# Decay exponents of a Mamba-2 layer made on ScalarE from running sums, instead of on TensorE from split rows

## The chip, the cores and the metric

One Trainium2 chip, one of its cores. The metric is the device time of one execution in microseconds. PE is TensorE, DVE is VectorE, ACT is ScalarE, POOL is GpSimd, SP the engine that issues most transfers.

## What is computed

A Mamba-2 block (1024 tokens = 4 batches of 256, 512 features, 128 heads of 64, 8 groups with a state of 128) and after it a quantised feed-forward block. What matters here, cut from the reference:

```python
A_dt = (dt * A).reshape(b, nc, CHUNK, H).transpose(0, 3, 1, 2)
A_cum = jnp.cumsum(A_dt, axis=-1)
L = jnp.exp(_segsum(A_dt))
Y_diag = jnp.einsum('bzlhn,bzshn,bhzls,bzshp->bzlhp', Cc, Bc, L, xch)
decay_states = jnp.exp(A_cum[..., -1:] - A_cum)
states = jnp.einsum('bzlhn,bhzl,bzlhp->bzhpn', Bc, decay_states, xch)
...
Y_off = jnp.einsum('bzlhn,bzhpn,bhzl->bzlhp', Cc, prev, jnp.exp(A_cum))
Y = (Y_diag + Y_off).reshape(b, s, H, P) + hs * D[None, None, :, None]
```

For each head, batch and chunk of 128 tokens one needs the matrix exp(sum_l - sum_s) for l >= s (a chunk with itself, called own below) and for the second chunk the same against the first chunk's tokens (past). It is multiplied with C.B, which all 16 heads of a group share, to M, and y = M times x.dt.

## The kernel before

The channels go in 64 tiles of 128 (2 heads each), 8 tiles to a group. Each engine runs its own program of `step`s (one a tile) and, after the 8 tiles of a group, a `window` (the group's output projection and the next group's B and C); semaphores tie the engines. There is no planner: on each engine the order is that in which the code is written, so an instruction that waits holds all behind it on its engine. `over_tiles` writes the loops out; inside a group two tiles make one loop body.

In the step of a tile PE transposes hs (`turn`, 2 halves), projects the next tile's hs and gate in four units of 12 matmuls of 512 columns (`unit`: 0 and 1 are hs, 2 and 3 the gate, each a half of the tokens; numbers are held as two fp32r parts, so three matmuls make one), makes the exponents (`exponents`, six matmuls of 512 columns, on rows that hold the running sums as three bf16 parts), and makes y (`y_first`, `y_second`, 16 and 32 matmuls of 128 columns as the profile counts them). ACT makes the last tap of the convolution (`tap3`), the tanh of each silu (`hs_tanh`, `gate_tanh`), the exponentials (`decay`, `decays`: for a chunk's own matrix a Relu first, which bounds the exponent, then Exp) and the upper parts of weights (`upper_pair`: casts of w_raw, two a tile; `wo_hi`). DVE does the other three taps (`conv_rest`), the products of the silus (`hs_silu`, `gate_silu`), x.dt (`times_dt`), M (`weigh`, six of 512 columns) and hs.D + y. POOL makes the lower parts of weights, gated, its squares and their sum.

The proj banks tie them: unit 2 of PE takes the bank of unit 0, and so waits until DVE has done `conv_rest(0)`; unit 0 of the next tile waits for `gate_silu(0)`. SP loads wo_raw when POOL has split the last one, then the rows, then the pair of w_raw.

Ahead of the first tile, dt is projected, turned, and put through softplus; PE sums dt.A (L808), ACT copies the sums and splits them with POOL into three bf16 parts (L592 to L612), SP stores these, and loads each tile's rows back.

## Time and profile before

| | |
|---|---|
| median of 3 runs | 1919.47 us (1918.16 to 1920.56) |
| profiled execution: its time, its span | 1918.38 us, 1916.6 us |
| PE busy | 1820.9 us, 95% |
| DVE busy | 1301.1 us, 68% |
| POOL busy | 1006.9 us, 53% |
| ACT busy | 918.7 us, 48% |
| granted TensorE clock, mean | 0.986 |

Busy time is what an engine's instructions take; the span runs from the first instruction to the last. Matmuls overlap in the pipeline, so PE's pace is read from their starts, not from their durations. The profile's page gives shares, its timeline the order in time, and its chain the work that ended last.

### The profile page before, as it was taken

Reading aid. Unit: us, or ns where it says so; the run is one execution under the profiler, and the core shown is the slowest. Engines: PE = TensorE matmul, PEld = TensorE weight load, DVE = VectorE, ACT = ScalarE, POOL = GpSimd, SP = SyncE. Lnnn points to the kernel's source line nnn. Section 1 sums busy time; section 2 is a strip of 40 time slices with the busy share of each in tenths; the row PEclk is TensorE's granted clock in tenths of the full one; section 3 lists DMA queues with packets and bytes.
Section 4 is the critical chain, followed back from the end, with each engine's and each line's share of the span. In section 5 each row is a group of like instructions: output and inputs, shape, how many; then the busy total and the mean of one; then the engine's idle time right before and its main releaser. Section 6 shows DMA issues by size and latency. Waiting matters only on the chain.

```text
span 1916.6 us, 37316 instructions
## 1 busy us (share of the span) xinstructions
PE 1820.9 (95%) x11192; PEld 1484.7 (77%) x11192; DVE 1301.1 (68%) x2149; ACT 918.7 (48%) x1660; POOL 1006.9 (53%) x802
## 2 busy tenths in 40 slices
PE   5799999999999999999999999999999977989898
PEld 4677787778777877787778777877887756878887
DVE  6588638863886388638863886388648857777776
ACT  3566536643664366436643664366436632212221
POOL 4266636663666366536653666366636665233220
PEclk9899999999999999999999999999999988999999
DMA  2211101110111011101110111011101110111101
GB/s 91 61 52 51 34 12 51 51 33 12 51 51 33 12 51 51 33 12 51 51 33 12 51 51 33 12 51 51 33 12 52 40 48 20 41 44 36 40 11 45
DMA packets 43639, 74.90 MB, mean 39 GB/s; under 512 B 10356, under 2 KB 11508, under 8 KB 43608
## 3 DMA queue, kind: packets, MB, share of 16 engines
q1 hardware_dynamic: 42600, 73.12, 12.1%
q10 hardware_dynamic: 1008, 1.38, 0.2%
...
q14 instruction: 14, 0.11, 0.0%
...
## 4 chain that ended last, share of the span: by engine, by line
PE 87%; DVE 8%; issue 2%; POOL 1%; ACT 1%; DVEq 0%; POOLq 0%; ACTq 0%
PE proj L743 15%; PE proj L745 15%; PE proj L744 15%; PE y L875 6%; PE y L929 6%; PE y L931 5%; PE y L930 5%; PE y L865 3%; PE trb L842 3%; PE diff L851 3%; DVE gated L1234 2%; PE misc L851 1%; PE y L743 1%; PE y L744 1%; PE y L745 1%
## 5 line engine op out<-in xcount | busy, mean ns | idle before, releaser
L743 PE MATMUL proj<-xhi,w_hi 128*128 128x512 f32 x1088 | 465.9, 428 | 5.6 <-DVE v L1057 5.6
L745 PE MATMUL proj<-xhi,w_lo 128*128 128x512 f32 x1088 | 425.9, 391 | 0.0
L744 PE MATMUL proj<-xlo,w_hi 128*128 128x512 f32 x1088 | 425.6, 391 | 0.0
L392 POOL TENSOR_TENSOR w_lo<-w_raw,w_hi 128x512 fp32r<-128x512 f32 x144 | 184.2, 1298 | 227.9 <-ACT w_hi L522 227.9
L1057 DVE SCALAR_TENSOR_TENSOR v<-proj,par_sb,v 128x510 f32<-128x510 f32 (+2 forms) x384 | 281.9, 741 | 15.0 <-ACT v L544 11.7
L448 POOL TENSOR_TENSOR g_lo<-gated,g_hi 128x512 fp32r<-128x512 f32 x128 | 164.8, 1290 | 190.4 <-ACT g_hi L675 189.8
L743 PEld LDWEIGHTS proj<-xhi,w_hi 128*128 128x128 f32 x1088 | 205.0, 188 | 75.2 <-issue 7.9
L745 PEld LDWEIGHTS proj<-xhi,w_lo 128*128 128x128 f32 x1088 | 204.8, 188 | 46.4
L744 PEld LDWEIGHTS proj<-xlo,w_hi 128*128 128x128 f32 x1088 | 205.4, 189 | 38.6
L1152 DVE TENSOR_TENSOR M<-diff,cb 128x512 f32<-128x512 f32 x256 | 170.1, 686 | 81.4 <-ACT diff L630 81.4
L929 PE MATMUL y<-wo_hi,g_hi 128*128 128x512 f32 x512 | 204.3, 399 | 5.5 <-POOL g_lo L448 5.1
L930 PE MATMUL y<-wo_lo,g_hi 128*128 128x512 f32 x512 | 201.2, 393 | 0.0
L931 PE MATMUL y<-wo_hi,g_lo 128*128 128x512 f32 x512 | 201.1, 393 | 0.0
L416 POOL TENSOR_TENSOR wo_lo<-wo_raw,wo_hi 128x512 f32 (+1 forms) x64 | 81.9, 1279 | 223.9 <-ACT wo_hi L658 223.9
L675 ACT CAST g_hi<-gated 128x512 fp32r<-128x512 f32 x128 | 78.6, 620 | 236.7 <-PE y L931 236.7
L544 ACT ACTIVATE v<-proj,par_sb 128x512 f32<-128x512 f32 x128 | 99.7, 779 | 188.6 <-PE proj L745 188.6
L626 ACT ACTIVATE diff<-diff 128x512 f32<-128x512 f32 x192 | 105.5, 579 | 136.9 <-PE diff L851 136.9
L1197 DVE SCALAR_TENSOR_TENSOR resid<-y,rg,resid 128x512 f32<-128x512 f32 x64 | 47.9, 749 | 170.5 <-PE y L931 169.0
L424 POOL TENSOR_TENSOR gated<-hs,gate 128x512 f32 (+1 forms) x128 | 162.7, 1292 | 0.4 <-DVE hs L1178 0.4
L438 POOL TENSOR_TENSOR sqacc<-sqacc,sq 128x512 f32<-128x512 f32 x128 | 162.6, 1291 | 0.0
L875 PEld LDWEIGHTS y<-M,xdt 128*64 128x64 f32 x2048 | 110.5, 137 | 25.5 <-issue 22.2
L875 PE MATMUL y<-M,xdt 128*64 128x128 f32 x2048 | 125.9, 276 | 2.8 <-DVE M L1152 2.8
...
## 6 DMA issues: line engine op xcount, KB each, us to landing
w_raw<-in_win SPq DMA_DIRECT2D x144, 256.0 KB, 2.7
wo_raw<-in_wout SPq DMA_DIRECT2D x64, 256.0 KB, 2.6
M<-in_w SPq DMA_DIRECT2D x14, 512.0 KB, 3.3
cb<-in_w SPq DMA_DIRECT2D x7, 512.0 KB, 3.3
...
out<-resid SPq DMA_DIRECT2D x8, 256.0 KB, 2.0
...
resid<-in_x SPq DMA_DIRECT2D x4, 256.0 KB, 4.6
```

Of the source, the lines that this page charges most:

```text
L392: e.tensor_tensor(w_lo[:, slot, i, :], w_raw[:, i, :], w_hi[:, slot, i, :].bitcast(F32), ALU.subtract).then_inc(split.sem, 1)
L424: e.tensor_tensor(gated[:, bass.ds(j, 1), h * HALF:(h + 1) * HALF], hs[:, par_:par_ + 1, h * HALF:(h + 1) * HALF], gate[:, par_:par_ + 1, ...
L448: e.tensor_tensor(g_lo[:, kk, :, :], gated[:, 4 * kk:4 * kk + 4, t * P:(t + 1) * P], g_hi[:, kk, :, :].bitcast(F32), ALU.subtract).then_in ...
L743: e.matmul(o, hi_l, hi_r, start=first, stop=False)
L744: e.matmul(o, hi_l, lo_r, start=False, stop=False)
L745: return e.matmul(o, lo_l, hi_r, start=False, stop=last)
L875: mm = e.matmul(ybank[b // 2][head * HD:(head + 1) * HD, (b % 2) * S + P:(b % 2 + 1) * S], xdt[:, 2 * b + part, head * HD:(head + 1) * HD] ...
L929: e.matmul(o, g_hi[:, kk, k, :], wo_hi[:, kt, :], start=first, stop=False)
L930: e.matmul(o, g_hi[:, kk, k, :], wo_lo[:, kt, :], start=False, stop=False)
L931: mm = e.matmul(o, g_lo[:, kk, k, :], wo_hi[:, kt, :], start=False, stop=last)
L1057: e.scalar_tensor_tensor(dst[:, :, d:S], src[:, :, 0:S - d], weights(K - 1 - d), dst[:, :, d:S], ALU.mult, ALU.add)\
L1152: e.tensor_tensor(M[:, SLOT[q], :], dbank[q % 3][:, :], cb[:, q // 2, :], ALU.mult)\
```

## The change

The running sums stay fp32 and go to HBM once; each tile gets two rows of them (one a head), each broadcast over 128 partitions by the transfer itself (`load_row`, 128 x 1024 fp32), and a block of 24 columns (`load_offset`) with each partition's own sum, for every block of 128 tokens. ACT forms the exponent as it reads the row: `decay_own` makes eight Relu of 128 columns with the offset as bias and one Exp over 1024 columns, `decay_past` four Exp of 128 columns with bias. PE's exponent matmuls go. DVE weighs an own matrix in one operation of 1024 columns. Head 0 of a tile is made and weighed a tile ahead (for a group's first tile, in the window before it), head 1 in the tile. y is one block after unit 1. The two own banks are now one tensor of 1024 columns. Ahead of the first tile B and C are projected before hs and gate, and the splitting of the sums is gone. POOL keeps one buffer of squares in place of two.

```diff
-        M = sb("M", [P, 4, HALF])
-        bc = M[:, :, :].rearrange("p (a u) f -> p a (u f)", a=2)
+        M = sb("M", [P, 6, HALF])
+        bc = M[:, 0:4, :].rearrange("p (a u) f -> p a (u f)", a=2)
+        M_own = [M[:, a:a + 2, :].rearrange("p a f -> p (a f)") for a in (0, 4)]
+        M_past = [M[:, 2, :], M[:, 3, :]]
...
+
+            def load_row(t, head):
+                sp.dma_start(row[:, head, :],
+                             sums[bass.ds(2 * t + head, 1), :].rearrange("a f -> (a f)").partition_broadcast(P))\
+                    .then_inc(s_row[head], 16)
+
+            def load_offset(t, par_):
+                sp.dma_start(offset[:, par_, :], offsets[:, bass.ds(t, 1), :].rearrange("p a k -> p (a k)"))\
+                    .then_inc(s_row[0], 16)
...
+            def step(g, j, par_, nxt, nxt2, ahead):
                 sp.wait_ge(wolo.sem, wolo.at(g, j, 0))
                 sp.dma_start(wo_raw[:, :], wout[TPG * g + j, :, :]).then_inc(woraw.sem, 16)
                 if nxt:
-                    sp.wait_ge(dready.sem, dready.at(g, j, 1))
-                    load_rows(TPG * g + j + 1, 1 - par_)
+                    sp.wait_ge(edone.sem, edone.at(g, j, 2))
+                    load_offset(TPG * g + j + 1, 1 - par_)
+                    load_row(TPG * g + j + 1, 0)
                 if nxt2:
                     load_pair(9 * g + j + 3, split.at(g, j, 0))
+                if nxt:
+                    sp.wait_ge(edone.sem, edone.at(g, j, 4))
+                    load_row(TPG * g + j + 1, 1)
 
...
+            def decay_own(g, j, par_, head):
+
+                act.wait_ge(s_row[head], (16 * TPG * (2 - head)) * g + (32 - 16 * head) * j + 16)
+                act.wait_ge(mdone.sem, mdone.at(g, j, 2 * head - 1))
+                for z in range(2):
+                    for b in range(B):
+                        block = 2 * b + z
+                        at = head * NB + block
+                        ins = e.activation(diff[z][:, b * P:(b + 1) * P], row[:, head, block * P:(block + 1) * P],
+                                           ACT.Relu, scale=-1.0, bias=offset[:, par_, at:at + 1])
+                ins.then_inc(dbound.sem, 1)
+                act.wait_ge(dbound.sem, dbound.at(g, j, head + 1))
+                e.activation(own[:, :], own[:, :], ACT.Exp, scale=-1.0).then_inc(edone.sem, 1)
+
+            def decay_past(g, j, par_, head):
+
+                act.wait_ge(mdone.sem, mdone.at(g, j, 2 * head))
+                for b in range(B):
+                    block = 2 * b + 1
+                    at = head * NB + 2 * B + b
+                    ins = e.activation(misc[:, b * P:(b + 1) * P], row[:, head, block * P:(block + 1) * P],
+                                       ACT.Exp, bias=offset[:, par_, at:at + 1])
+                ins.then_inc(edone.sem, 1)
+
+            act.wait_ge(s_off, 6)
+            act.wait_ge(cbd.sem, cbd.at(0, 0, 0))
+            decay_own(0, 0, 0, 0)
+            decay_past(0, 0, 0, 0)
+
+            def step(g, j, par_, nxt, nxt2, ahead):
+                decay_own(g, j, par_, 1)
+                decay_past(g, j, par_, 1)
                 w = tile_weights(TPG * g + j + 1)
                 if nxt:
                     tap3(0, w, ready.at(g, j, 1), silu.at(g, j, -1))
-                decay(2)
-                decay(3)
+                if nxt2:
+                    act.wait_ge(ready.sem, ready.at(g, j, 0))
+                    upper_pair(par_, 9 * g + j + 3)
                 if nxt:
                     tap3(1, w, ready.at(g, j, 2), silu.at(g, j, 0))
                     act.wait_ge(gdone.sem, gdone.at(g, j, 0))
                     hs_tanh(hs[:, 1 - par_, :], 0, taken.at(g, j, 1))
-                if nxt2:
-                    act.wait_ge(ready.sem, ready.at(g, j, 0))
-                    upper_pair(par_, 9 * g + j + 3)
-                decays(4)
+                if ahead:
+                    decay_own(g, j + 1, 1 - par_, 0)
                 if nxt:
                     hs_tanh(hs[:, 1 - par_, :], 1, taken.at(g, j, 2))
+                if ahead:
+                    decay_past(g, j + 1, 1 - par_, 0)
+                if nxt:
                     gate_tanh(gate[:, 1 - par_, :], 0, ready.at(g, j, 3))
                 act.wait_ge(woraw.sem, woraw.at(g, j, 16))
                 act.wait_ge(gused.sem, gused.at(g, 0, 0))
                 e.activation(wo_raw[:, :], wo_raw[:, :], ACT.Copy,
                              scale=par_sb[:, bass.ds(TPG * g + j, 1), K + 2:K + 3].rearrange("p a b -> p (a b)"))\
                     .then_inc(woscaled.sem, 1)
-                if nxt:
-                    gate_tanh(gate[:, 1 - par_, :], 1, ready.at(g, j, 4))
                 act.wait_ge(woscaled.sem, woscaled.at(g, j, 1))
                 e.copy(wo_hi[:, bass.ds(j, 1), :].rearrange("p a f -> p (a f)"), wo_raw[:, :])\
                     .then_inc(wohi.sem, 1)
+                if nxt:
+                    gate_tanh(gate[:, 1 - par_, :], 1, ready.at(g, j, 4))
                 if not nxt:
 
                     for h in range(2):
                         act.wait_ge(gdone.sem, gdone.at(g, j, h + 1))
-                        act.wait_ge(sacc.sem, sacc.at(g, j, h - 1))
-                        e.activation(sq[:, h:h + 1, :], gated[:, bass.ds(j, 1), h * HALF:(h + 1) * HALF],
-                                     ACT.Square).then_inc(sqs.sem, 1)
+                        act.wait_ge(sacc.sem, sacc.at(g, j, h))
+                        e.activation(sq[:, :], gated[:, bass.ds(j, 1), h * HALF:(h + 1) * HALF]
+                                     .rearrange("p a f -> p (a f)"), ACT.Square).then_inc(sqs.sem, 1)
 
             def window(g, nxt):
...
@@ -683,6 +679,10 @@
                     bc_tile(g + 1, 1, ready.window(g, 0), taken.window(g, 0), silu.window(g, 0))
                 for i in range(2, 16):
                     g_upper(i)
+                    if i == 12 and nxt:
+                        act.wait_ge(cbd.sem, cbd.at(g + 1, 0, 0))
+                        decay_own(g + 1, 0, 0, 0)
+                        decay_past(g + 1, 0, 0, 0)
                     if i == 7 and nxt:
...
 
             def first_unit(n):
 
+
                 pair, piece, h = n // 4, (n // 2) % 2, n % 2
 
-                free = (None, None, 1, 2, None, None, 3, 4)[n]
-                project(pair, piece, h, 2 * pair + piece + 1, free, bc_banks[0][piece] if pair else proj)
...
+                def y():
+                    pe.wait_ge(mdone.sem, mdone.at(g, j, 4))
                     pe.wait_ge(xdts.sem, xdts.at(g, j, 2))
                     pe.wait_ge(ysum.sem, ysum.at(g, j, 0))
                     pe.wait_ge(oadded.sem, oadded.at(g, 0, 0))
                     for b in range(B):
-                        for head in range(2):
-                            mm = e.matmul(ybank[b // 2][head * HD:(head + 1) * HD, (b % 2) * S:(b % 2) * S + P],
-                                          xdt[:, 2 * b, head * HD:(head + 1) * HD],
-                                          M[:, SLOT[head], b * P:(b + 1) * P], start=True, stop=True)
-                    mm.then_inc(yready.sem, 1)
-
...
+
+                        for z, part in ((0, 0), (1, 0), (1, 1)):
                             for head in range(2):
+                                weights = M_past[head][:, cols] if z > part else \
+                                    M_own[head][:, after_own if z else cols]
                                 mm = e.matmul(
-                                    ybank[b // 2][head * HD:(head + 1) * HD, (b % 2) * S + P:(b % 2 + 1) * S],
-                                    xdt[:, 2 * b + part, head * HD:(head + 1) * HD],
-                                    M[:, SLOT[2 + 2 * part + head], b * P:(b + 1) * P],
-                                    start=(part == 0), stop=(part == 1))
+                                    ybank[b // 2][head * HD:(head + 1) * HD,
+                                                  (b % 2) * S + z * P:(b % 2) * S + (z + 1) * P],
+                                    xdt[:, 2 * b + part, head * HD:(head + 1) * HD], weights,
+                                    start=(part == 0), stop=(part == z))
                         if b % 2:
                             mm.then_inc(yready.sem, 1)
 
                 turn(0)
-
-                pe.wait_ge(s_rowq[par_], (TPG * 32) * g + 32 * j + (64 - 32 * par_))
-                pe.wait_ge(cbd.sem, cbd.at(g, 0, 0))
-                exponents(0)
-                exponents(1)
                 if nxt:
                     unit(0)
                 turn(1)
-                exponents(2)
-                exponents(3)
                 if nxt:
                     unit(1)
-                y_first()
-                exponents(4)
-                exponents(5)
+                y()
                 if nxt:
                     unit(2)
                     unit(3)
-                y_second()
 
             def window(g, nxt):
...
+            def weigh_own(g, j, head):
+                dve.wait_ge(edone.sem, edone.at(g, j, 2 * head + 1))
+                if head == 0:
+                    dve.wait_ge(cbd.sem, cbd.at(g, 0, 0))
+                    dve.wait_ge(yready.sem, yready.at(g, j, 0))
+                e.tensor_tensor(M_own[head], own[:, :], cb[:, 0:2, :].rearrange("p a f -> p (a f)"), ALU.mult)\
+                    .then_inc(mdone.sem, 1)
+
+            def weigh_past(g, j, head):
+                dve.wait_ge(edone.sem, edone.at(g, j, 2 * head + 2))
+                e.tensor_tensor(M_past[head], misc[:, :], cb[:, 2, :], ALU.mult).then_inc(mdone.sem, 1)
+
+            weigh_own(0, 0, 0)
+            weigh_past(0, 0, 0)
+            gate_silu(gate[:, 0, :], 0, 7)
+            gate_silu(gate[:, 0, :], 1, 8)
+
+            def step(g, j, par_, nxt, nxt2, ahead):
                 t = TPG * g + j
                 y = hs[:, par_, :]
 
@@ -1143,40 +1150,30 @@
                     scale = dt[:, 4 * h:4 * h + 4, bass.ds(2 * t, 2)].unsqueeze(3).broadcast_to([P, 4, 2, HD])
                     e.tensor_tensor(dst, src, scale, ALU.mult).then_inc(xdts.sem, 1)
 
...
                 times_dt(0)
-                weigh(0)
-                weigh(1)
+                weigh_own(g, j, 1)
                 times_dt(1)
-                if nxt:
-                    conv_rest(0, w, tap.at(g, j, 1), convs.at(g, j, 0),
-                              (lambda: weigh(2), lambda: weigh(3)))
+                weigh_past(g, j, 1)
+                if nxt:
+                    conv_rest(0, w, tap.at(g, j, 1), convs.at(g, j, 0))
                     conv_rest(1, w, tap.at(g, j, 2), convs.at(g, j, 2),
                               (lambda: hs_silu(hs[:, 1 - par_, :], 0, tanh.at(g, j, 1)),))
-                else:
-                    weigh(2)
-                    weigh(3)
-                weigh(4)
-                weigh(5)
+                if ahead:
+                    weigh_own(g, j + 1, 0)
                 if nxt:
                     hs_silu(hs[:, 1 - par_, :], 1, tanh.at(g, j, 2))
                     gate_silu(gate[:, 1 - par_, :], 0, tanh.at(g, j, 3))
+                if ahead:
+                    weigh_past(g, j + 1, 0)
+                skip = tile_weights(t)
+                for h in range(2):
+
+                    dve.wait_ge(yready.sem, yready.at(g, j, h + 1))
+                    e.scalar_tensor_tensor(halves(y, h), halves(y, h), skip(K + 1), ybank[h][:, :],
+                                           ALU.mult, ALU.add).then_inc(ysum.sem, 1)
+                if nxt:
                     gate_silu(gate[:, 1 - par_, :], 1, tanh.at(g, j, 4))
-                own = tile_weights(t)
-                for h in range(2):
-
-                    dve.wait_ge(yready.sem, yready.at(g, j, h + 2))
-                    e.scalar_tensor_tensor(halves(y, h), halves(y, h), own(K + 1), ybank[h][:, :],
-                                           ALU.mult, ALU.add).then_inc(ysum.sem, 1)
 
             def window(g, nxt):
                 if nxt:
@@ -1198,6 +1195,9 @@
                                            ALU.mult, ALU.add).then_inc(oadded.sem, 1)
                     if t == 3 and nxt:
                         cbs_kept(cbr.window(g, 1))
+                    if t == 6 and nxt:
+                        weigh_own(g + 1, 0, 0)
+                        weigh_past(g + 1, 0, 0)
                     if not nxt:
                         dve.wait_ge(oadded.sem, oadded.window(g, t + 1))
                         moments(t)
```

ACT's program, in the middle of a step (hs is the tile's silu input, v the convolution, diff and misc the exponents' banks). Before, it reads:

```order
L555 ACTIVATE hs<-v 128x512
L644 REGISTER_ALU
L521 ISA
L522 CAST w_hi<-w_raw 128x512 x2
L625 REGISTER_ALU
L626 ACTIVATE diff<-diff 128x512
L625 REGISTER_ALU
L626 ACTIVATE misc<-misc 128x512
L629 REGISTER_ALU
L630 ACTIVATE diff<-diff 128x512
L629 REGISTER_ALU
L630 ACTIVATE misc<-misc 128x512
```

and in the changed kernel, from the same hs tanh (L535 here), where own and misc are the exponents' banks and row and offset their sources:

```order
L535 ACTIVATE hs<-v 128x512
L598 ISA
L599 ISA
L604 ACTIVATE own<-row,offset 128x128 x8
L607 ISA
L608 ACTIVATE own<-own 128x1024
L535 ACTIVATE hs<-v 128x512
L612 REGISTER_ALU
L616 ACTIVATE misc<-row,offset 128x128 x4
L538 REGISTER_ALU
L539 ACTIVATE gate<-proj 128x512
```

The casts of w_raw have moved from behind the first hs tanh to a place ahead of the second tap; behind that tanh now stand the nine activations of the next tile's head 0, with its past block behind the second hs tanh.

DVE's program from the start of a step: M products, x.dt and the first conv steps. Before:

```order
L1152 TENSOR_TENSOR M<-diff,cb 128x512
L1138 REGISTER_ALU
L1144 ISA
L1144 TENSOR_TENSOR xdt<-trb,dt 128x512
L1052 ISA
L1057 ISA
L1057 SCALAR_TENSOR_TENSOR v<-proj,par_sb,v 128x2x255
L1147 REGISTER_ALU
L1152 TENSOR_TENSOR M<-misc,cb 128x512
L1056 ISA
L1057 ISA
L1057 SCALAR_TENSOR_TENSOR v<-proj,par_sb,v 128x2x254
```

and in the changed kernel:

```order
L1151 TENSOR_TENSOR xdt<-trb,dt 128x512
L1124 ISA
L1128 TENSOR_TENSOR M<-own,cb 128x1024
L1145 REGISTER_ALU
L1151 ISA
L1151 TENSOR_TENSOR xdt<-trb,dt 128x512
L1132 REGISTER_ALU
L1133 TENSOR_TENSOR M<-misc,cb 128x512
L1036 ISA
L1041 ISA
L1041 SCALAR_TENSOR_TENSOR v<-proj,par_sb,v 128x2x255
```

Before, M products stand between the conv steps of half 0; now both of head 1 (1024 and 512 columns) stand ahead of the first of them, with `times_dt(1)` between.

SP's transfers of a step. Before:

```order
L305 ISA
L306 ISA
L306 DMA wo_raw<-in_wout 128x512
L308 ISA
L281 ISA
L281 DMA row_r<-rows_r 3x2048
L283 ISA
L283 DMA row_l<-rows_l 4x768
L283 ISA
L283 DMA row_l<-rows_l 4x768
L283 ISA
L283 DMA row_l<-rows_l 4x768
```

and in the changed kernel:

```order
L286 ISA
L286 DMA offset<-offsets 128x24
L281 ISA
L281 DMA row<-sums 128x1024
L273 ISA
L274 ISA
L274 DMA w_raw<-in_win 128x512
L273 REGISTER_ALU
L274 ISA
L274 DMA w_raw<-in_win 128x512
L309 REGISTER_ALU
L281 ISA
L281 DMA row<-sums 128x1024
```

Four small loads have given way to the offset block and a row ahead of the w_raw pair, and a second row behind it.

## Rows read from the trace of the kernel before

**Rows 1.** The page's first part: busy us, share of the span, instructions.
```profile
PE 1820.9 (95%) x11192; PEld 1484.7 (77%) x11192; DVE 1301.1 (68%) x2149; ACT 918.7 (48%) x1660; POOL 1006.9 (53%) x802
```

**Rows 2.** PE's timeline in one tile: start us, us, engine, line, operation, count.
```profile
912.56 0.66 PE L842 MATMUL trb<-ident,hs 128*128 128x128 f32 x4
...
920.98 0.39 PE L851 MATMUL diff<-row_r,row_l 128*128 128x512 bf16 x1
...
921.65 0.40 PE L744 MATMUL proj<-xlo,w_hi 128*128 128x512 f32 x1
```

**Rows 3.** The chain that ended last: start us, us, what; the y matmuls of two tiles.
```profile
97.45 1.90 PE y L875 x32
...
195.63 1.90 PE y L875 x32
```

**Rows 4.** ACT's timeline in the tile that PE begins at 912.56.
```profile
916.97 0.78 ACT L544 ACTIVATE v<-proj,par_sb 128x512 f32<-128x512 f32 x1 [1.45 <-PE proj L745]
917.65 0.59 ACT L620 ACTIVATE misc<-misc 128x512 f32<-128x512 f32 x1
...
921.80 1.13 ACT L522 CAST w_hi<-w_raw 128x512 fp32r<-128x512 f32 x2
...
924.30 0.56 ACT L630 ACTIVATE misc<-misc 128x512 f32<-128x512 f32 x1
924.78 0.63 ACT L555 ACTIVATE hs<-v 128x512 f32<-128x512 f32 x1
925.30 0.60 ACT L559 ACTIVATE gate<-proj 128x512 f32<-128x512 f32 x1
925.78 0.73 ACT L652 ACTIVATE wo_raw<-wo_raw,par_sb 128x512 f32<-128x512 f32 x1
```

**Rows 5.** ACT's timeline ahead of the first tile: 128 and 1024 columns.
```profile
25.73 0.31 ACT L532 ACTIVATE sq<-sq 128x128 f32<-128x128 f32 x1
...
34.87 1.06 ACT L567 ACTIVATE gated<-gated 128x1024 f32<-128x1024 f32 x1
35.83 0.76 ACT L544 ACTIVATE v<-proj,par_sb 128x512 f32<-128x512 f32 x1
```

**Rows 6.** DVE's timeline: three conv steps in a row, and two M products.
```profile
39.21 2.31 DVE L1057 SCALAR_TENSOR_TENSOR v<-proj,par_sb,v 128x510 f32<-128x510 f32 x3
...
924.50 0.69 DVE L1152 TENSOR_TENSOR M<-diff,cb 128x512 f32<-128x512 f32 x1 [0.44 <-ACT diff L630]
925.11 0.68 DVE L1152 TENSOR_TENSOR M<-misc,cb 128x512 f32<-128x512 f32 x1
```

**Rows 7.** Timelines of ACT, POOL, DVE and PE late in one window.
```profile
1030.13 0.62 ACT L675 CAST g_hi<-gated 128x512 fp32r<-128x512 f32 x1 [2.10 <-PE y L931]
1032.85 0.62 ACT L675 CAST g_hi<-gated 128x512 fp32r<-128x512 f32 x1 [2.10 <-PE y L931]
...
1030.83 1.28 POOL L448 TENSOR_TENSOR g_lo<-gated,g_hi 128x512 fp32r<-128x512 f32 x1 [1.44 <-ACT g_hi L675]
...
1032.94 0.75 DVE L1197 SCALAR_TENSOR_TENSOR resid<-y,rg,resid 128x512 f32<-128x512 f32 x1 [4.69 <-PE y L931]
...
1038.10 0.60 PE L842 MATMUL trb<-ident,hs 128*128 128x128 f32 x4
```

**Rows 8.** PE's timeline ahead of the first tile and in it.
```profile
75.98 0.77 PE L824 MATMUL diff<-M 128*128 128x128 f32 x2 [11.14 <-DVE M L1071]
...
80.95 0.60 PE L842 MATMUL trb<-ident,hs 128*128 128x128 f32 x4
83.24 0.60 PE L851 MATMUL diff<-row_r,row_l 128*128 128x512 bf16 x2 [1.68 <-DVE cb L1127]
```

**Rows 9.** SP's timeline in the tile of 912.56; transfers: KB, median us to landing.
```profile
916.24 0.98 SPq L275 DMA_DIRECT2D w_raw<-in_win  x2
...
w_raw<-in_win SPq DMA_DIRECT2D x144, 256.0 KB, 2.7
...
M<-in_w SPq DMA_DIRECT2D x14, 512.0 KB, 3.3
```

298 lines of the change are left out of this document (121 added, 177 removed).

## Prediction

> **What bounds the kernel now.** First the page's busy shares [rows 1]: TensorE (PE) is busy 95% of the span, VectorE (DVE) 68%, ScalarE (ACT) 48%, so a first look says that only PE's own work counts. Then PE's timeline in one tile [rows 2]: its pieces follow each other without a gap. From the first exponent matmul at 920.98 to the second matmul of the next projection at 921.65 are 0.67 us for two exponents and one 512-column projection matmul; twelve of those take 2.72 in the stretch of [rows 7], 0.23 each, so two exponents cost 0.44. Then the chain that ended last [rows 3]: six tiles between 97.45 and 195.63 give **16.36 us a tile**. ACT and DVE have slack inside it: but the question for this change is how much, since it puts work on ACT.
>
> **What it takes from PE.** Six exponent matmuls a tile, 3 x 0.44 = 1.32 us, and one of the two seams around the y matmuls, about 0.1. The 24 y matmuls stay. PE alone would need 16.36 - 1.42 = 14.95 us a tile.
>
> **What it puts on ACT.** Gone are ten 512-column activations. They come at 0.48 to 0.52 us from start to start (924.30, 924.78, 925.30 in [rows 4]), 4.95 us in all. New are 24 activations of 128 columns with a bias from SBUF (16 Relu, 8 Exp) and two Exp of 1024.
>
> The slot s of a small one is the number on which everything hangs, and before has none like it. From rows: a Tanh from SBUF has a slot of 0.52 (924.78 to 925.30), and 1024 columns have 0.96 (34.87 to 35.83, [rows 5]), so 384 columns fewer are 0.33 less: 0.19. An operand pointer costs extra: the Identity with scale and bias from SBUF has 0.68 (916.97 to 917.65), 0.20 over the plain 0.48 from PSUM, so 0.10 each. s = 0.19 + 0.10 = **0.29**. Lower bound: the plain fixed part may be that of the Exps on PSUM (0.48 less 0.43 for the columns, 0.05), then s = 0.11 + 0.05 + 0.10 = 0.26, and 0.25 with a cheaper pointer. Upper bound: the one 128-column activation of before lasts 0.31 us [rows 5]; with the pointer and no overlap 0.41, with 0.09 of overlap 0.32. I take 0.29, since both of its parts come from back-to-back rows.
>
> The Trainium skill (ScalarE: Activation LUTs, What ACT_TABLE_LOAD costs) gives 280 ns + 0.833 ns a column with a pointer bias, and about 93 ns of overlap back to back; that is an estimate of 0.294 us for this instruction, by which the sum below would be some 4 us longer. The rows of before have no such instruction to confirm it.
>
> ACT's content is then: the rest of a tile (two taps 0.68, two hs tanh 0.52, two casts of w, two gate tanh 0.48, the wo scaling 0.76 and cast 0.52) 5.6, plus 24 x 0.29 = 7.0, plus 2 x 0.92 (an Exp of 0.48 with 0.43 more columns), plus 0.12 twice, where Exp waits for the last Relu of its own and the overlap is lost: **14.7 us**. That alone nearly fills 14.95, and ACT also waits.
>
> **The ring.** One path now goes round once a tile, by the order in which the code stands. Head 1: Relus 2.32 + 0.12; Exp 0.99 and 0.10 to reach DVE; weigh_own of 1024 columns 1.14 (a 512-column one has 0.61, 924.50 to 925.11; at most twice that, 1.22, and 0.07 or so of it is fixed, [rows 6]); times_dt 0.60; weigh_past 0.60; then the three conv steps of half 0, which nothing interleaves any more, 2.31 [rows 6] and 0.10 back to ACT; hs tanh 0.52; head 0 of the next tile: Relus 2.32 + 0.12, Exp 0.92; hs tanh 0.52; four past Exps 1.16; gate tanh 0.48; wo scaling 0.76, wo cast 0.52; gate tanh 0.50; the loop's branch and registers 0.10; and head 1 of the next tile. Sum **16.20 us**, = 10.40 + 20 s. PE is not on it: its units 2 and 3 wait for the conv results, its y for weigh_past. So the steady tile goes from 16.36, bound by PE, to 16.20, bound by ACT and DVE in turn. What covered ACT's work before was PE's length; it is used up.
>
> Not every tile pays the ring. In a window ACT and DVE are idle much of the time; head 0 of the coming tile is made there, and head 1 can start when DVE has weighed it: the output addition at 1032.94 [rows 7] + 0.75 + 1.14 = 1034.9, 3.2 us ahead of the tile's start at 1038.10. The first tile of a group therefore goes at PE's 14.95, the second at about 15.35 (the lead is used up in it: its tap waits for PE's unit 0), six at 16.20. A group: 127.5 against 8 x 16.36 = 130.9, **-3.4 x 8 = -27 us**.
>
> **The window.** ACT casts one g_hi per 2.72 us (1030.13 to 1032.85), POOL's half ends at 1030.83 + 1.28 = 1032.11, and PE wants it at 1032.85 - 0.1: 0.6 of slack [rows 7]. Between the 13th and the 14th cast now stand head 0's activations, 12 x 0.29 + 0.12 + 0.92 = 4.5. The 14th comes at 0.53 + 4.5 = 5.0 instead of 2.72, PE stands 1.7 to 1.8: **+12.5 us** in seven windows.
>
> **Ahead of the first tile.** B and C are now projected first, the exact three-part split (three rounds of casts, negations and POOL subtractions) and its twelve stores are gone. Before, PE waits 11.14 us for B and C and begins C.B at 75.98; the tile's first projection starts after 83.24, at 83.5 [rows 8]. After, DVE's queue sets it. From 39.21 [rows 6]: two half convs 4.44, two steps of the dt chain at 1.25 (1024 columns and the wait for each other) 2.5, two silus 1.3, the clip 0.7 and the product with A 1.25, which gives 49.4; C's convs 4.44 and silus 1.3, 55.1; a wait of 0.4 for v; hs convs 4.44, 60.0. C.B at its old length (80.95 - 75.98), 65.2; three copies and lags 67.2; ACT's head 0 3.5 and lag, 70.8; weigh_own 1.14, weigh_past 0.6, gate silu 0.6: 73.2. That is the unit's start, **-10.3 us**. POOL's memsets of the rows fall away ahead of the first norm too, which may give 1 or 2 us more; they are not in the sum. The row and offset transfers (issued near 58 to 64) are hidden by the C.B part; without that cover they would cost 3 to 5 us once.
>
> **DMA.** Each tile now loads two rows over 128 partitions, 512 KB each, and a small offset block, in place of four small loads. SP's order matters: wo_raw, offset, row of head 0, then the pair of w_raw, which before was issued at 916.24, 3.7 us into its tile, and landed 2.7 later [rows 9]. ACT's casts of it stood 9.2 us into the tile (921.80) and are moved ahead of the second tap. Now wo_raw is issued when POOL has split the previous tile's wo, whose cast ends about 1.2 us into the tile: + 1.3 + 0.4 = 2.9; w_raw at 4.9 and 5.4; behind 512 KB (3.3 to land against 2.7 for 256 KB, [rows 9], so 0.6 for each further 256 KB) it lands at 8.0 and 8.6. The casts then end near 9.1 and the tap near 9.8, where hs tanh would start by the ring at 9.8. So it is hidden, with nothing to spare: I cost it at 0. The second row (issued 6.3, needed at the tile's end) has about 7 us. POOL keeps its work and its slack.
>
> The last stage is unchanged. Sum: -27 + 12.5 - 10.3 = -25, from the profiled execution's own 1918.4 (span 1916.6, median of the runs 1919.5, 1.1 above it): **1893 us**.
>
> **The rivals.**
> *PE stays the bound* (s at 0.23 or less, or shorter waits than I sum). For: PE's rows without gaps, and s is derived, not seen. Against: all rows on pointers and on SBUF sources. 64 x -1.42 = -91, windows +6, ahead -10: 1823. Chance 0.12; the ground between it and the forecast (s near 0.25, tile 15.4: -0.8 x 48, with the second tiles and windows -45) gives 1848, 0.18.
> *w_raw comes late, slower than before.* The casts stand ahead of the second tap in ACT's queue; if the second piece lands x later than 8.7 us into the tile, tap, hs tanh and everything behind them shift by x, and all but the first tiles pay, 56 x. At x = 0.5 the gain is gone; at x = 1, 1893 + 56 = 1949. For: 1.3 MB in a burst on one queue, a row read 128 times from the same 4 KB. Against: the landing times of before, at low DMA load [rows 9]. Chance 0.10.
> *The small activations are slower than 0.31* (no full overlap when each reads a pointer): s = 0.32 gives a tile of 16.8, +0.6 x 48 + 2: 1924; s = 0.41, 2010. Chance 0.10.
> *No net change*, ring and windows eating the gain ahead of the first tile: 1916 to 1923, 0.06, at s = 0.31 to 0.32.
>
> **How the numbers follow.** The forecast with its own spread (s 0.27 to 0.305, 0.1 of lags in the ring, 1870 to 1910) has 0.44. Each 0.01 us of s moves the time by 10 us, each 0.1 us of wait in the ring by 5. The range leaves out the PE-bound end and the far slow end: 1843 to 1928. 0.2% (3.8 us) is what a measurement of this kernel tells from no change. Faster: 0.12 + 0.18 + 0.44 + a share of the slower cases that end below = 0.78; same 0.06; slower 0.16.
>
> **What would show it.** ACT busy over 80%, with 128-column activations at 0.36 to 0.39 us each and 0.29 from start to start; PE under 93%, waiting once a tile for DVE (y for M, or a transpose for xdt) by 1.2 us in all, in tiles 3 to 8 of a group and not in the first; a stand of 1.8 us before the 14th block of a window; the first projection of tile 0 near 73. ACT waiting for the transfer of w_raw would be the second rival. I am wrong if s is off by more than 0.02, if ACT does not overlap such small instructions, or if the loads come late.

## The result, and the profile after

The changed kernel takes **1985.47 us** (median of 4 runs, 1981.3 to 1989.02), before 1918.82 in the same comparison: ratio 1.0351, 95% interval 1.0331 to 1.037. It is slower by 3.5%, where 1893 us was predicted, and lies outside the range of 1843 to 1928. Its profiled execution has a span of 1986.9 us at a granted clock of 0.983.

The page's busy shares, waits and transfers, in the form of [rows 1, 9]. First the page's first part and its part on the chain:

```profile
PE 1771.1 (89%) x10816; PEld 1447.3 (73%) x10816; DVE 1305.6 (66%) x2021; ACT 1165.4 (59%) x2682; POOL 996.1 (50%) x792
...
PE 17%; DVE 7%; ACT 6%; issue 4%; DMA 3%; POOL 2%; SPq 1%; ACTq 0%; DVEq 0%; POOLq 0%
DMA w_raw<-in_win 3%; PE proj L743 2%; PE proj L745 2%; PE proj L744 2%; ACT own L604 2%; PE y L913 2%; PE y L914 2%; PE y L915 2%; DVE gated L1234 2%; PE y L743 1%; PE y L744 1%; PE y L745 1%; POOL wo_lo L397 1%; PE own L966 1%; ACT misc L616 1%
```

One row of its waits (total us, times, longest us), then three of its transfers (KB, median us from issue to landing):

```profile
ACT w_hi L502 <- DMA w_raw<-in_win: 154.9, 55, 3.4
...
row<-sums SPq DMA_DIRECT2D x128, 512.0 KB, 5.0
w_raw<-in_win SPq DMA_DIRECT2D x144, 256.0 KB, 4.9
wo_raw<-in_wout SPq DMA_DIRECT2D x64, 256.0 KB, 2.6
```

The first row is ACT's casts of w_raw waiting for its transfer: 55 times, 2.8 us each. The transfer that landed 2.7 us after its issue now takes 4.9. ACT is busy for 59% of the span, where over 80% was named as a sign; what that says stands further down. ACT's timeline in one tile:

```profile
904.19 2.41 ACT L604 ACTIVATE own<-row,offset 128x128 f32<-128x128 f32 x8
...
916.10 0.77 ACT L524 ACTIVATE v<-proj,par_sb 128x512 f32<-128x512 f32 x1
919.75 1.26 ACT L502 CAST w_hi<-w_raw 128x512 fp32r<-128x512 f32 x2 [2.88 <-DMA w_raw<-in_win]
920.91 0.77 ACT L524 ACTIVATE v<-proj,par_sb 128x512 f32<-128x512 f32 x1
921.59 0.62 ACT L535 ACTIVATE hs<-v 128x512 f32<-128x512 f32 x1
922.11 2.40 ACT L604 ACTIVATE own<-row,offset 128x128 f32<-128x128 f32 x8
924.54 1.01 ACT L608 ACTIVATE own<-own 128x1024 f32<-128x1024 f32 x1
925.46 0.62 ACT L535 ACTIVATE hs<-v 128x512 f32<-128x512 f32 x1
925.98 1.23 ACT L616 ACTIVATE misc<-row,offset 128x128 f32<-128x128 f32 x4
927.15 0.58 ACT L539 ACTIVATE gate<-proj 128x512 f32<-128x512 f32 x1
927.63 0.71 ACT L648 ACTIVATE wo_raw<-wo_raw,par_sb 128x512 f32<-128x512 f32 x1
928.47 0.62 ACT L652 CAST wo_hi<-wo_raw 128x512 f32 x1
```

and SP's issues and POOL's split of wo ahead of them, and the turns of PE at the start of this tile:

```profile
912.85 0.33 SPq L301 DMA_DIRECT2D wo_raw<-in_wout  x1
913.53 0.33 SPq L286 DMA_DIRECT2D offset<-offsets  x1
914.06 0.33 SPq L281 DMA_DIRECT2D row<-sums  x1
914.82 0.93 SPq L274 DMA_DIRECT2D w_raw<-in_win  x2
916.34 0.33 SPq L281 DMA_DIRECT2D row<-sums  x1
...
911.38 1.30 POOL L397 TENSOR_TENSOR wo_lo<-wo_raw,wo_hi 128x512 f32 x1 [6.34 <-ACT wo_hi L652]
...
909.95 0.60 PE L849 MATMUL trb<-ident,hs 128*128 128x128 f32 x4
913.71 0.66 PE L849 MATMUL trb<-ident,hs 128*128 128x128 f32 x4
```

The tile begins at 909.95. wo_raw goes 2.90 into it (2.9 forecast), w_raw 4.87 (4.9). But the first cast starts at 9.80, not 8.0. From here the rows close to a ring, a path that goes round once a tile and so sets its length. It has none of DVE's work in it: the cast of wo (928.47) lets POOL split it, POOL lets SP load the next wo_raw, and only behind that wait stand the row and the w_raw pair, which ACT's casts wait for, with the second tap, the tanh, head 0, and the next cast of wo behind them. One tile of it is 904.19 to 922.11 at L604, 17.9 us (its neighbours take 17.4 to 18.0); the prediction had 16.20.

### The profile page after: what moved, and what is told of

The parts are those of the page before. It is cut to its first block and busy times, and to the rows that moved or that the text cites. A ratio compares the mean times of both kernels' runs of the same rounds, so it can differ in the third digit from the quotient of the medians.

```text
span 1986.9 us, 36002 instructions
## 1 busy us (share of the span) xinstructions
PE 1771.1 (89%) x10816; PEld 1447.3 (73%) x10816; DVE 1305.6 (66%) x2021; ACT 1165.4 (59%) x2682; POOL 996.1 (50%) x792
## 5 line engine op out<-in xcount | busy, mean ns | idle before, releaser
L743 PE MATMUL proj<-xhi,w_hi 128*128 128x512 f32 x1080 | 450.7, 417 | 87.7 <-DVE v L1041 79.1
L1041 DVE SCALAR_TENSOR_TENSOR v<-proj,par_sb,v 128x510 f32<-128x510 f32 x378 | 280.2, 743 | 116.3 <-ACT v L524 95.9
L604 ACT ACTIVATE own<-row,offset 128x128 f32<-128x128 f32 x1024 | 307.7, 355 | 11.3 <-DVE M L1128 9.1
L1128 DVE TENSOR_TENSOR M<-own,cb 128x1024 f32<-128x1024 f32 x128 | 156.6, 1224 | 133.0 <-ACT own L608 133.0
L913 PE MATMUL y<-wo_hi,g_hi 128*128 128x512 f32 x512 | 204.5, 399 | 16.2 <-POOL g_lo L428 15.8
L869 PE MATMUL y<-M,xdt 128*64 128x128 f32 x3072 | 184.4, 277 | 34.8 <-DVE M L1133 34.8
L869 PEld LDWEIGHTS y<-M,xdt 128*64 128x64 f32 x3072 | 169.8, 138 | 60.1 <-DVE xdt L1151 29.2
L502 ACT CAST w_hi<-w_raw 128x512 fp32r<-128x512 f32 x144 | 87.4, 619 | 156.8 <-DMA w_raw<-in_win 154.9
```

Of the source, the lines that this page charges most:

```text
L604: ins = e.activation(diff[z][:, b * P:(b + 1) * P], row[:, head, block * P:(block + 1) * P], ACT.Relu, scale=-1.0, bias=offset[:, par_, at ...
L743: e.matmul(o, hi_l, hi_r, start=first, stop=False)
L869: mm = e.matmul(ybank[b // 2][head * HD:(head + 1) * HD, (b % 2) * S + z * P:(b % 2) * S + (z + 1) * P], xdt[:, 2 * b + part, head * HD:(h ...
L913: e.matmul(o, g_hi[:, kk, k, :], wo_hi[:, kt, :], start=first, stop=False)
L1041: e.scalar_tensor_tensor(dst[:, :, d:S], src[:, :, 0:S - d], weights(K - 1 - d), dst[:, :, d:S], ALU.mult, ALU.add)\
```

## The experiments

Each run is beside before (1917.9 to 1918.5 us). Edits are against the changed kernel where nothing else is said. A code line `...` marks lines left out. A tile's length is read in a steady stretch around 900 us, from one start of head 0's first Relu, or of PE's turn, to the next.

**e1_pair_first: the w_raw pair ahead of offset and row.**

```diff
                 sp.dma_start(wo_raw[:, :], wout[TPG * g + j, :, :]).then_inc(woraw.sem, 16)
+                if nxt2:
+                    load_pair(9 * g + j + 3, split.at(g, j, 0))
                 if nxt:
...
                     load_row(TPG * g + j + 1, 0)
-                if nxt2:
-                    load_pair(9 * g + j + 3, split.at(g, j, 0))
```

> The changed kernel with the w_raw pair issued ahead of the offset block and the row of head 0; nothing else. Theory A (the excess over the forecast is the wait of ACT's casts for w_raw, 2.4 to 3.1 us a tile, because 512 KB of row stand ahead of it on the queue): the pair is issued 1.3 us sooner with only wo_raw ahead, the casts no longer wait, a tile is 16.2 to 16.4 us and the time 1890 to 1905. Rival B (the whole burst slows every transfer, the order doesn't matter): ACT then waits for the row of head 0 instead, a tile stays at 17.3 to 17.9, the time at 1950 to 1985.

1918.92 us, ratio 1.000 (0.999 to 1.0011), between the two ranges, so neither theory is right by itself. w_raw lands after 2.9 now, but the row after 5.3, and head 0 meets it: ACT waits 23 times, 16.4 us in all, for the row. Tiles take 16.6 to 17.9. 67 of the 92 us that the prediction missed come from the order of two issues.

**e2_short_rows: rows for 4 partitions only.** The other partitions keep what the first tile left in them: the output is another one.

```diff
-                sp.dma_start(row[:, head, :],
-                             sums[bass.ds(2 * t + head, 1), :].rearrange("a f -> (a f)").partition_broadcast(P))\
+                sp.dma_start(row[0:4, head, :], sums[bass.ds(2 * t + head, 1), :].rearrange("a f -> (a f)").partition_broadcast(4))\
                     .then_inc(s_row[head], 16)
```

> The changed kernel, but each tile's row goes to 4 partitions only (16 KB instead of 512 KB); the first tile's rows are left in the other partitions, so the decays of later tiles are not the reference's. All instructions of the engines stay. Theory A: w_raw lands 2.7 us after its issue as in the kernel before, no wait, tile 16.2, time 1890 to 1900. Rival C (the ring of ACT and DVE is itself longer than the 16.2 us that was summed, and the wait for w_raw only fills slack in it): 1940 or more although no transfer is waited for.

1900.03 us, 0.9907 (0.989 to 0.9924). w_raw lands after 2.7, as in [rows 9]. ACT's wait for it is not gone, but small:

```profile
ACT w_hi L502 <- DMA w_raw<-in_win: 28.7, 59, 2.8
```

That is 0.5 us each time, and it is slack: ACT's timeline, the start of head 0 in four tiles:

```profile
891.73 2.40 ACT L604 ACTIVATE own<-row,offset 128x128 f32<-128x128 f32 x8
...
908.10 2.40 ACT L604 ACTIVATE own<-row,offset 128x128 f32<-128x128 f32 x8
...
924.45 2.40 ACT L604 ACTIVATE own<-row,offset 128x128 f32<-128x128 f32 x8
...
940.80 2.40 ACT L604 ACTIVATE own<-row,offset 128x128 f32<-128x128 f32 x8
```

16.36 a tile, the same as in e5_loads_early below, where no such wait is left. This is the length of the prediction's ring, 0.16 more than it had; that it is that ring, e7_both_orders bears out.

**e3_distinct_rows: the same bytes from 128 different rows.** Each partition reads a row of its own, so the exponents are other ones and so is the output.

```diff
-                sp.dma_start(row[:, head, :],
-                             sums[bass.ds(2 * t + head, 1), :].rearrange("a f -> (a f)").partition_broadcast(P))\
-                    .then_inc(s_row[head], 16)
+                sp.dma_start(row[:, head, :], sums[:, :]).then_inc(s_row[head], 16)
```

> The changed kernel, but each row transfer reads 128 different rows of the sums, one for each partition, instead of one row 128 times: the same bytes and the same piece size; the decays are not the reference's. If it is the bytes ahead on the queue that delay w_raw, the landing times stay at 5 us and the time at 1980 to 1990. If it is the repeated reading of one 4 KB row, the row lands in 3.3 us like the other 512 KB loads of the kernel, w_raw about 1.7 us sooner, and the time is 1900 to 1915.

1954.82 us, 1.0194 (1.0177 to 1.0211). The page's medians are 4.6 instead of 5.0 for the rows and 4.3 instead of 4.9 for the pair; they mix both heads' rows and the windows. In the steady tiles alone head 0's row lands after 4.4 instead of 5.0, the two pieces of the pair after 4.3 and 4.4 instead of 5.1. ACT waits for w_raw 61 times, 2.0 us each. So reading one source row 128 times costs 0.6 us of the row's landing and 0.7 of the pair's. The time is 31 us less than the change's, and the late load as a whole costs 86 (e5_loads_early); the rest of the delay is there with distinct rows too. Neither theory holds alone.

**e4_cast_later: ACT's casts of w_raw back behind the first hs tanh.**

```diff
-                if nxt2:
-                    act.wait_ge(ready.sem, ready.at(g, j, 0))
-                    upper_pair(par_, 9 * g + j + 3)
                 if nxt:
...
                     hs_tanh(hs[:, 1 - par_, :], 0, taken.at(g, j, 1))
+                if nxt2:
+                    act.wait_ge(ready.sem, ready.at(g, j, 0))
+                    upper_pair(par_, 9 * g + j + 3)
```

> The changed kernel with ACT's two casts of w_raw back behind the first hs tanh, where they stood in the kernel before; the transfers are as in the change. The casts then stand on the ring (16.2 + 1.0 = 17.2 us a tile) but start some 10.4 us into the tile, when w_raw has landed. By the ring: 1940 to 1950, with no wait of the casts. If ACT had slack there instead (no ring): 1890 to 1900.

1956.06 us, 1.0196 (1.0179 to 1.0213), tile 17.40. The wait for w_raw is gone, but the two casts stand behind the tanh, on the ring, 1.03 longer for it, while ACT stands idle for 1.88 us ahead of the tanh:

```profile
906.15 0.63 ACT L535 ACTIVATE hs<-v 128x512 f32<-128x512 f32 x1 [1.88 <-DVE v L1041]
```

The landing time is unchanged (5.0). The expectation had 1940 to 1950, from a ring of 16.2; it is 16.36 + 1.03.

**e5_loads_early: the wait for POOL's split behind the other loads.**

```diff
-                sp.wait_ge(wolo.sem, wolo.at(g, j, 0))
-                sp.dma_start(wo_raw[:, :], wout[TPG * g + j, :, :]).then_inc(woraw.sem, 16)
                 if nxt:
                     sp.wait_ge(edone.sem, edone.at(g, j, 2))
...
                     load_pair(9 * g + j + 3, split.at(g, j, 0))
+                sp.wait_ge(wolo.sem, wolo.at(g, j, 0))
+                sp.dma_start(wo_raw[:, :], wout[TPG * g + j, :, :]).then_inc(woraw.sem, 16)
```

> The changed kernel with all rows in full, but SP's transfers of a step in another order: the offset block and the row of head 0 (their buffers are free since the last tile), the pair of w_raw, and only then the wait for POOL and wo_raw. Theory A (the ring went through SP: wo cast, POOL's split of wo, SP's wait for it, and the w_raw that stands behind): the w_raw and the row have landed long before ACT wants them, the same bytes move, a tile is 16.35 us as with the short rows, the time 1896 to 1906. Rival (the 64 MB of rows cost by themselves, through the memories' ports): 1915 or more.

1899.79 us, 0.9906 (0.9889 to 0.9924), tile 16.36, as with short rows. Its transfers, then SP's issue of the pair and PE's turn ahead of it:

```profile
row<-sums SPq DMA_DIRECT2D x128, 512.0 KB, 3.8
w_raw<-in_win SPq DMA_DIRECT2D x144, 256.0 KB, 4.2
...
899.47 0.93 SPq L274 DMA_DIRECT2D w_raw<-in_win  x2
...
898.51 0.61 PE L849 MATMUL trb<-ident,hs 128*128 128x128 f32 x4
```

All bytes are moved, w_raw still takes 4.2 us, and it costs nothing, because SP issues it 0.96 us into the tile (899.47, after PE's turn at 898.51) instead of 4.87. The edit does two things: the issue comes 3.9 us sooner, and wo_raw no longer stands ahead of the row, which with the pair lands 0.8 sooner. The casts stood for 2.8 us, so the second alone would not have been enough.

**e6_dve_order: DVE's and ACT's order at head 1,** with the loads left as in the change.

```diff
                 times_dt(0)
-                weigh_own(g, j, 1)
                 times_dt(1)
-                weigh_past(g, j, 1)
+                weigh_own(g, j, 1)
                 if nxt:
-                    conv_rest(0, w, tap.at(g, j, 1), convs.at(g, j, 0))
+                    conv_rest(0, w, tap.at(g, j, 1), convs.at(g, j, 0), (lambda: weigh_past(g, j, 1),))
...
                 decay_own(g, j, par_, 1)
-                decay_past(g, j, par_, 1)
                 w = tile_weights(TPG * g + j + 1)
                 if nxt:
                     tap3(0, w, ready.at(g, j, 1), silu.at(g, j, -1))
+                decay_past(g, j, par_, 1)
```

> The changed kernel with its own order of transfers; on DVE both x.dt products stand ahead of weigh_own, and weigh_past between the conv steps of half 0; on ACT the first tap stands ahead of the past exponents. That shortens the path ACT - DVE - ACT by about 0.6 to 0.9 us. Theory A: that path is not the one that binds, the w_raw ring is (wo cast 0.8 to POOL, 1.3, SP 2.1, landing 4.9, casts 1.2, tap 0.7, tanh 0.5, head 0 3.4, tanh 0.5, past 1.2, gate 0.5, wo scaling 0.8: 17.9), which holds no DVE work: 1980 to 1990, as the change. Rival C (the ACT - DVE path binds): 1930 to 1950.

1988.2 us, 1.0368 (1.0349 to 1.0386). No gain: shortening the ring over DVE gives nothing while the ring over w_raw binds.

**e7_both_orders: the edits of e5_loads_early and e6_dve_order together.**

> Both of the two edits before: transfers early, and the order on DVE and ACT. With w_raw out of the way the ACT - DVE ring of the forecast binds, and now each tenth off it counts: a tile at 15.4 to 15.8 instead of 16.35, time 1860 to 1875. If ACT's own work (14.7 us) or PE's (14.95) binds already at 16.35, no gain over the transfers alone: 1895 to 1905.

1874.61 us, 0.978 (0.9762 to 0.9797). What was worth nothing alone is worth 25 us here. PE's timeline, turns of two tiles and the y between them:

```profile
887.16 0.60 PE L849 MATMUL trb<-ident,hs 128*128 128x128 f32 x4
...
891.33 2.84 PE L869 MATMUL y<-M,xdt 128*64 128x128 f32 x48 [0.79 <-DVE M L1133]
...
902.91 0.60 PE L849 MATMUL trb<-ident,hs 128*128 128x128 f32 x4
```

15.75 in this tile (15.63 to 15.75 in its neighbours), 0.79 of it PE's stand at y for weigh_past; 15.75 less 0.79 is the 14.95 of the prediction.

**e8_window_spread: on e7_both_orders, head 0 in the window in four pieces,** behind casts 10 to 13. `decay_own` is cut into `decay_bound` (the eight Relu, or four of them) and `decay_exp`.

```diff
-                    if i == 12 and nxt:
+                    if i == 10 and nxt:
                         act.wait_ge(cbd.sem, cbd.at(g + 1, 0, 0))
-                        decay_own(g + 1, 0, 0, 0)
+                        decay_bound(g + 1, 0, 0, 0, (0,))
+                    if i == 11 and nxt:
+                        decay_bound(g + 1, 0, 0, 0, (1,))
+                    if i == 12 and nxt:
+                        decay_exp(g + 1, 0, 0)
+                    if i == 13 and nxt:
                         decay_past(g + 1, 0, 0, 0)
```

> The kernel with both orders, and in the window head 0 of the coming tile is made in four pieces, behind the casts 10, 11, 12 and 13 (four Relu, four Relu, Exp, four past Exp: each at most 1.3 us), instead of in one piece of 4.5 us behind cast 12. PE's stand of 1.7 us there should go, seven times: 11 to 12 us less than the kernel with both orders, 1848 to 1864. If other casts are then late instead (each piece over the slack of 0.6), less than half of that.

1889.35 us, 0.9845 (0.982 to 0.9869): 15 us worse, a miss. ACT's timeline, then PE's, in one window:

```profile
997.53 1.24 ACT L604 ACTIVATE own<-row,offset 128x128 f32<-128x128 f32 x4 [6.86 <-DVE cb L1127]
...
1000.72 0.79 PE L925 MATMUL y<-wo_hi,g_hi 128*128 128x512 f32 x1 [2.57 <-POOL g_lo L428]
```

The first piece waits for DVE's masked copies of C.B, which come only after the time of cast 11, and holds casts 11 and 12 behind it.

**e9_window_later: the same four pieces behind casts 11 to 14.**

```diff
-                    if i == 10 and nxt:
+                    if i == 11 and nxt:
                         act.wait_ge(cbd.sem, cbd.at(g + 1, 0, 0))
...
-                    if i == 13 and nxt:
+                    if i == 14 and nxt:
                         decay_past(g + 1, 0, 0, 0)
```

> On top of the run with both orders (1874.6): the first tile's head 0 at the seven boundaries is cut in four pieces, behind casts 11, 12, 13 and 14 of g_hi, one cast later than in the run before it, where the first piece stood 6.9 us for the masked C.B copies. Theory (each piece hides behind PE's 4.6 us pair of matmuls; only the wait for cb was at fault): the stand of 1.7 us at each boundary goes, 7 x 1.7 = 12, so 1862 (1858 to 1870). Rival (ACT is late for PE in the window whatever the order, or the cb copies still end behind cast 11): 1874 or above.

1865.06 us, 0.9723 (0.9707 to 0.9739), the fastest that leaves nothing out: 9.5 of the 12 us, within the expected range. ACT's timeline in a window:

```profile
985.02 1.25 ACT L604 ACTIVATE own<-row,offset 128x128 f32<-128x128 f32 x4 [4.14 <-DVE cb L1127]
986.21 0.60 ACT L678 CAST g_hi<-gated 128x512 fp32r<-128x512 f32 x1
```

ACT still stands for cb, which holds cast 12, but PE no longer feels it: its stand of 1.66 us is gone in all seven windows. (The seven waits for g_lo of 0.6 us that are left lie some 27 us earlier in the window, and are in the runs before it too.) A group is 185.46 long instead of 187.11, 7 x 1.65 = 11.6, the whole of the 12; the rest up to the 9.5 measured lies behind the last tile, in the last stage, which these two traces show with 384.2 and 380.6 us though nothing was changed there.

**e10_one_bias: on e7_both_orders, two Relu of 512 columns with one bias each.** The other blocks get the offset of one, so the output is another one.

```diff
                 for z in range(2):
-                    for b in range(B):
-                        block = 2 * b + z
-                        at = head * NB + block
-                        ins = e.activation(diff[z][:, b * P:(b + 1) * P], row[:, head, block * P:(block + 1) * P],
-                                           ACT.Relu, scale=-1.0, bias=offset[:, par_, at:at + 1])
+                    at = head * NB + z
+                    ins = e.activation(diff[z][:, 0:B * P], row[:, head, z * B * P:(z + 1) * B * P],
+                                       ACT.Relu, scale=-1.0, bias=offset[:, par_, at:at + 1])
```

> On top of the run with both orders (1874.6), for the price of a bias for each block: the eight Relu of 128 columns of a head become two of 512 columns with one bias each, so seven of eight blocks get another block's offset (the output is another one). A head falls from 8 x 0.30 = 2.4 us to about 2 x 0.6 = 1.2, 2.4 a tile for two heads. If small activations set the tile (ACT's ring, 15.7 a tile): PE's own 14.95 binds, 0.75 x 63 = 47 less, 1827 (1820 to 1845). If DVE sets it (PE waits for M at y): the time stays within 10 of 1874.6.

1866.6 us, 0.973 (0.9713 to 0.9746). ACT loses 121 us of busy time and the kernel 8; the two Relu take 1.30 us against 2.40 for eight. The tile keeps its 15.65, with PE still standing at y (a window's late stand, then a tile's):

```profile
993.80 0.50 PE L911 MATMUL y<-wo_hi,g_hi 128*128 128x512 f32 x1 [0.56 <-POOL g_lo L428]
...
1009.49 2.84 PE L867 MATMUL y<-M,xdt 128*64 128x128 f32 x48 [0.83 <-DVE M L1131]
```

The 8 us are those of the windows: the stand there is 0.56 instead of 1.66, 7 x 1.1. So once DVE's order is mended, the bias for each block no longer sets the tile.

**e11_past_first: on e9_window_later, weigh_past directly behind weigh_own,** ahead of the convolution, and ACT's past block ahead of the tap.

```diff
                 decay_own(g, j, par_, 1)
+                decay_past(g, j, par_, 1)
                 w = tile_weights(TPG * g + j + 1)
                 if nxt:
                     tap3(0, w, ready.at(g, j, 1), silu.at(g, j, -1))
-                decay_past(g, j, par_, 1)
...
                 weigh_own(g, j, 1)
+                weigh_past(g, j, 1)
                 if nxt:
-                    conv_rest(0, w, tap.at(g, j, 1), convs.at(g, j, 0), (lambda: weigh_past(g, j, 1),))
+                    conv_rest(0, w, tap.at(g, j, 1), convs.at(g, j, 0))
```

> Against the run of the four window pieces behind casts 11 to 14 (1865.1). In it and in the run with one bias PE stands 0.7 to 0.85 us a tile at y, waiting for weigh_past, which stands behind a conv step; that wait and ACT's ring (head 1 at 884.89, hs tanh at 892.64, next head 1 15.7 later, without a gap but 0.75 ahead of the tanh) are both 15.7 long. Here only weigh_past is moved: directly behind weigh_own, ahead of the convolution, with ACT's past block ahead of the tap. PE's path gets 0.6 shorter, ACT's and DVE's ring keeps its content. Theory (two rings of equal length): tile 15.7 as before, 1865 (1860 to 1870), PE's stand moves from y to unit 2 or to the turn. Rival (only the path over y binds): tile 15.1, 1831 to 1840.

1883.66 us, 0.9812 (0.9795 to 0.9829): slower by 19, outside what either theory gave. PE's stand at y is gone, but the tile is 16.0. ACT's and DVE's timelines:

```profile
888.52 2.40 ACT L604 ACTIVATE own<-row,offset 128x128 f32<-128x128 f32 x8
...
893.05 0.77 ACT L524 ACTIVATE v<-proj,par_sb 128x512 f32<-128x512 f32 x1
...
896.64 0.63 ACT L535 ACTIVATE hs<-v 128x512 f32<-128x512 f32 x1 [1.12 <-DVE v L1053]
...
893.99 0.75 DVE L1053 SCALAR_TENSOR_TENSOR v<-proj,par_sb,v 128x510 f32<-128x510 f32 x1
```

The tanh comes 8.12 after head 1's first Relu, against 7.75 in e7_both_orders: the tap stands behind the past block, and the convolution waits for both it and weigh_past. I had counted DVE's work only.

**e12_past_first_one_bias: the edits of e11_past_first and e10_one_bias together.** The output is another one, as with e10_one_bias.

> The same order, and two Relu of 512 columns with one bias each in place of eight of 128 (the output is another one), on the window of four pieces. Both rings are now shortened, so PE's own tile should bind: 14.95 instead of 15.65, 0.7 x 56 = 39 under 1865: 1826 (1820 to 1835). Rival (something else holds the tile at 15.6, since one bias alone gave 15.65): 1860 to 1866.

1861.54 us, 0.9705 (0.9689 to 0.9721), where 1826 was expected: a miss, the rival's time. PE's timeline and DVE's:

```profile
877.97 0.66 PE L859 MATMUL trb<-ident,hs 128*128 128x128 f32 x4
...
887.66 0.50 PE L753 MATMUL proj<-xhi,w_hi 128*128 128x512 f32 x1 [0.33 <-DVE v L1051]
...
893.82 0.66 PE L859 MATMUL trb<-ident,hs 128*128 128x128 f32 x4
...
886.09 1.51 DVE L1051 SCALAR_TENSOR_TENSOR v<-proj,par_sb,v 128x508 f32<-128x508 f32 x2
```

15.85 a tile, and ACT waits in several places of it. From the second turn (877.97) DVE makes xdt, both M of head 1, the conv of half 0, the silu of hs, and the conv of half 1, which ends at 887.6; that frees the bank of unit 3 (887.66), and 6.16 later PE is at the next second turn. 9.69 + 6.16 is the tile. This third ring, over PE and DVE, is 0.1 to 0.2 longer than the two of e7_both_orders. One piece of it is not like the others, the silu of hs:

```profile
884.41 1.75 DVE L1065 SCALAR_TENSOR_TENSOR hs<-hs,v 128x512 f32<-128x512 f32 x1
```

In the tiles of this trace it takes 1.5 to 1.8 us in all 54 cases in which POOL was in the middle of its split of w_raw when it began, and 0.68 to 0.70 in the 73 in which POOL was idle. Here it ends at 886.16, 0.54 after the first of the two splits (884.33, 1.29 long). At 0.69 the ring would be 14.8, and PE's 14.95 would bind. No run moves POOL's split away to test it.

## Why the prediction was wrong

**The step that failed** is the one under DMA: "lands at 8.0 and 8.6 ... hidden, with nothing to spare: I cost it at 0". The issue times in it held (2.90 and 4.87 against 2.9 and 4.9). So did the 0.6 for each 256 KB piece behind the row. What was mis-sized is the landing of the row itself. 8.0 and 8.6 are what comes out when the row, issued near 4.1, lands 3.3 later, as 512 KB did with nothing around them [rows 9], and each piece 0.6 behind it. In the tile above the row is issued at 4.11 and lands 4.96 later, at 9.07, and the pieces 0.7 and 0.6 behind that, at 9.78 and 10.42: 1.8 later than forecast.

Where the row's 1.7 come from, medians of single transfers of head 0's row show. With distinct source rows and no wo_raw just ahead of it (the first tiles of the groups in e3_distinct_rows) it takes 3.4. With the repeated source in the same place, 4.3 in the changed kernel and 4.2 in e5_loads_early. With wo_raw ahead, 4.4 for distinct rows and 5.0 for the repeated one. So wo_raw's 256 KB ahead cost 0.7 to 1.0 us, and the repeated source 0.6 to 0.9. The sum had neither; they are the two reasons that the prediction gave for its second rival.

The rival that I gave 0.10 is what happened, at its own price: the second piece lands at 10.4, 1.7 to 1.8 beyond the 8.7 of the rival, and 1893 + 56 x 1.7 = 1988. Having written "nothing to spare" beside a price of 0, I should have given that rival far more.

**Why it was so dear.** The delay is not absorbed anywhere, since the landing closes a ring of its own. The e5_loads_early run, which takes SP's wait for POOL out of that ring (and wo_raw out of the front of the burst), gives back 85.7 us, 56 x 1.53, with all bytes still moved. That the ring is closed over w_raw and not over DVE, e6_dve_order shows: less work on DVE's path changed nothing. e1_pair_first shows the same burst from the other end: what is issued second comes late.

**What held, as the runs without the late load show it.** The slot of the small activation was forecast as 0.29: eight of them take 2.40 us from the first's start to the last's end, 355 ns for one, so (2.40 - 0.355) / 7 = 0.292. By this case's trace the estimate of 0.294 us from the Trainium skill (ScalarE: Activation LUTs, What ACT_TABLE_LOAD costs) is right too. ACT's content: 14.7 us a tile forecast, 14.72 busy in a tile of e5_loads_early. The ring: 16.20 forecast, 16.36 in two runs; the convolution and its way to ACT take 2.64 of it in e5_loads_early (906.00 to 908.64) against the 2.41 summed, and smaller terms give 0.07 back. That leaves 48 x 0.16 = 7.7 us, and e5_loads_early at 1899.8 is 7 above the forecast of 1893. The first tile of a group: 14.95, measured 14.80 (1081.74 to 1096.54); the second: 15.35, measured 15.60 in e5_loads_early. These two nearly cancel. The window and the start ahead of the first tile stand in PE's timeline of the changed kernel:

```profile
1070.26 0.50 PE L913 MATMUL y<-wo_hi,g_hi 128*128 128x512 f32 x1 [1.66 <-POOL g_lo L428]
...
71.28 0.80 PE L743 MATMUL proj<-xhi,w_hi 128*128 128x512 f32 x1 [7.54 <-DVE gate L1060]
```

1.66 against 1.7 to 1.8, and 71.28 against 73.2 (74.16 in e5_loads_early, so the start is good to 2 us only). e9_window_later confirms the cost of the window: a group is 1.65 shorter without that stand.

One sign was set wrongly, apart from the miss: "ACT busy over 80%". By the prediction's own terms ACT is busy for 64 x 14.7 = 941 us in the tiles and for some 240 elsewhere (918.7 - 64 x 10.6 before), which is 62% of 1893. e5_loads_early shows 61%, though ACT fills 90% of its steady tile. So the 59% of the changed kernel says nothing against the ring; a page's share is an average over tiles, windows and the last stage.

**The rivals that did not come.** PE does not stay the bound: no run, not even e12_past_first_one_bias with its 24 activations cut to 12, comes below 15.6 in a steady tile. The small activations are not slower than 0.31.

**What stays open.** Whether a steady tile can come down to 14.95 with any order wasn't settled: three rings of 15.65 to 16.0 were seen, and each edit that shortened one lengthened or uncovered another. The long silu in e12_past_first_one_bias is the one piece in sight whose normal length would do it. Why a repeated source row, or 256 KB ahead on the queue, costs what it does, no run shows; the traces only size them.
